# Second attention's routing steps behind the output, first expert slot loaded early, expert halves turned by DMA

## The reference

```
x = x + L1_xattn(_layernorm(x), ctx, ctx, Wq, bq, Wk, bk, Wv, bv, Wo)   # 16 heads of 64, 77 keys
x_flat = _layernorm(x).reshape(4096, 512)
topk_logits, topk_idx = top_k(x_flat @ moe_router, 2)                  # 8 experts, 2 per row
w = softmax(topk_logits)
x_sort = x_flat[token_ids_sort]                                        # rows sorted by expert
gate, up = split(ragged_dot(x_sort, moe_w13, group_sizes), 2)          # 512 -> 2 x 1024
out = ragged_dot(silu(gate) * up, moe_w2, group_sizes)                 # 1024 -> 512
x = x + zeros_like(x_flat).at[token_ids_sort].add(out * w_sort)
```

## Time and profile before

| | us |
|---|---|
| median of 3 runs | 2937.68 |
| lowest, highest | 2935.63, 2941.66 |
| the profiled execution's own time | 2946.32 |
| its span | 2944.4 |

### The profile page before, as it was taken

How to read it: one execution, slowest core, us unless ns; L and a number is a source line. 1 busy time by engine, 2 the same in 40 slices (tenths; PEclk the granted TensorE clock), 3 DMA queues, 4 the chain that set the end, 5 groups by cost and what they waited for, 6 DMA issues and landing times. The chain is left out here.

```text
span 2944.4 us, 45924 instructions
## 1 busy us (share of the span) xinstructions
PE 2430.0 (83%) x15743; PEld 1294.0 (44%) x15923; DVE 1664.0 (57%) x2533; ACT 1027.2 (35%) x1676; POOL 1094.7 (37%) x934
## 2 busy tenths in 40 slices
PE   8799944666656698888888499999999999999960
PEld 5566621222222265555555244444444444444430
DVE  4599878899898465555657442333333434342235
ACT  2365635788876444444445111111111111111100
POOL 0244412777767112323225650060633505330026
PEclk9799976889888799999999699999999999999985
DMA  6300013344333200111112331141322413231128
GB/s 238 120 2 2 2 58 118 130 177 164 118 118 118 75 10 10 38 38 34 38 48 80 111 108 36 29 120 30 114 78 75 118 32 97 74 82 29 36 83 277
DMA packets 181491, 240.15 MB, mean 82 GB/s; under 512 B 99110, under 2 KB 102182, under 8 KB 180854
## 3 DMA queue, kind: packets, MB, share of 16 engines
q1 hardware_dynamic: 158325, 158.73, 16.6%
q0 software_dynamic: 23040, 79.72, 8.7%
HBM read 101.77 MB, written 118.03 MB: 75 GB/s over the span
## 5 line engine op out<-in xcount | busy, mean ns | idle before, releaser
L2015 PE MATMUL e_gate_up<-weights,e_x_t 128*128 x3335 | 751.2, 380 | 28.1 <-DMA e_x_t<-sorted_x 23.9
L2015 PEld LDWEIGHTS e_gate_up<-weights,e_x_t 128*128 128x128 bf16 x3408 | 328.2, 98 | 394.7 <-issue 27.2
L2089 DVE TENSOR_TENSOR e_mid<-e_gate,e_gate_up 128x512 f32<-128x512 f32 x142 | 97.6, 687 | 574.1 <-ACT e_gate L2066 574.1
L2036 PE MATMUL e_out<-weights,e_mid_t 128*128 x1669 | 377.4, 379 | 4.3 <-issue 2.5
L2066 ACT ACTIVATE e_gate<-e_gate_up 128x512 f32<-128x512 f32 x142 | 84.8, 597 | 716.8 <-PE e_gate_up L2015 716.8
L2036 PEld LDWEIGHTS e_out<-weights,e_mid_t 128*128 128x128 bf16 x1704 | 166.7, 98 | 203.4 <-issue 2.9
L843 POOL TENSOR_TENSOR a_e<-a_e,a_total 128x616 f32<-128x616 f32 x64 | 76.4, 1214 | 405.6 <-DVE a_total L1202 405.6
L1510 POOL TENSOR_TENSOR f_shared<-f_shared 128x512 f32<-128x512 f32 x128 | 181.0, 1415 | 123.5 <-DVE f_shared L1788 123.5
L1580 PE MATMUL f_out<-f_w,hidden 128*128 128x512 f16 x512 | 141.3, 402 | 96.8 <-ACT hidden L1682 95.9
L1968 POOL TENSOR_TENSOR e_token<-e_token 1x1 f32<-1x1 f32 x6 | 1.1, 183 | 565.7 <-PE e_out L2036 565.7
L1499 POOL TENSOR_TENSOR hidden<-hidden,f_up_row 128x512 f32<-128x512 f32 x128 | 178.2, 1402 | 86.6 <-ACT f_up_row L1711 86.6
(11 more groups left out here) (262 smaller groups left out, 4089.9 us busy)
## 6 DMA issues: line engine op xcount, KB each, us to landing
sorted_x<-f_zero_row SPq DMA_DIRECT2D x8, 8448.0 KB, 24.1
raw_weights<-in_w POOLq DMA_DIRECT2D x88, 512.0 KB, 4.0
sorted_y<-e_y_rows SPq DMA_DIRECT2D x71, 256.0 KB, 2.0
x<-in_x SPq DMA_DIRECT2D x4, 2048.0 KB, 21.7
out<-x SPq DMA_DIRECT2D x32, 256.0 KB, 4.1
hidden<-in_w_t SPq DMA_DIRECT2D x1, 4096.0 KB, 17.3
f_shared<-in_w_t SPq DMA_DIRECT2D x1, 4096.0 KB, 13.3
weights<-in_w SPq DMA_DIRECT2D x6, 512.0 KB, 3.6
```

The costliest lines, as they stand in the source:

```text
L2015: last = nc.tensor.matmul(gate_up[half][:, part, :], x_t[:, u, a, k, :], plan.weights13[:, bass.ds(expert % 2, 1), b, k, col:col + 512], s ...
L2036: last = nc.tensor.matmul(out[:, :], mid_t[:, a, j, :], plan.weights2[:, bass.ds(expert % 2, 1), b, j, :], start=(j == 0 and a == b == 0), ...
L2089: nc.vector.tensor_tensor(mid[:, half, :], gate[:, half, :], gate_up[half][:, 1, :], ALU.mult).then_inc(mid_made, 1)
```

## The change

In `attention1` counts and partial logits come behind the output on TensorE; counts, while flips are made (before step `TAIL`), also behind the flips. Rows of all but the last two groups are turned, chosen and counted a step later than before (`begin`), while moments and norms keep their step. ScalarE normalises the rows ahead of the copy of the partial logits. VectorE adds the output before it does the routing's arithmetic, and `rows_of` copies the counts from PSUM into `counted` first, so that the bank is free at once.

The memory of the keys and of the turned expert rows is one (`plan.keys`, `plan.x_t`). SP issues the load of slot 0's rows at the end of `attention1`, once all scatters have landed; `experts` begins with the load of slot 1.

In `experts` TensorE no longer turns the middle. SP turns each half (128 x 1024 bf16, both parts) by a DMA transpose from `mid_parts` to `mid_t`, which has a second buffer (`mid_turn`). SP's order in slot s is: rows of slot s+2, results of slot s-1, the two halves of slot s. ScalarE copies the output of slot s-1 after VectorE has finished both halves of slot s, and VectorE waits for the turn of a half in the slot before ahead of overwriting it.

```diff
@@ -701,12 +703,14 @@
         for g, tiles in enumerate(GROUPS):
+            begin = tiles[-1] + (5 if g < len(GROUPS) - 2 else 4)
             norms_at[tiles[-1] + 4] = g
             for j in range(0, len(tiles), 2):
-                pairs_at[tiles[-1] + 4 + j // 2] = tiles[j]
-            choice_at[tiles[-1] + 4 + len(tiles) // 2] = g
-            rows_at[tiles[-1] + 5 + len(tiles) // 2] = g
+                pairs_at[begin + j // 2] = tiles[j]
+            choice_at[begin + len(tiles) // 2] = g
+            rows_at[begin + 1 + len(tiles) // 2] = g
         STEPS = NT + 6
+        TAIL = NT + 3
         groups_of = {t: g for g, tiles in enumerate(GROUPS) for t in tiles}
@@ -795,6 +799,11 @@
+            for i in range(SENT):
+                sp.wait_ge(sent_out[i], 32 * LATE // SENT)
+            sp.wait_ge(late_out, 32 * (NT - LATE))
+            sp.dma_start_transpose(out=plan.x_t[:, 0, :, :, :].rearrange("p a k n -> p (a k) n"),
+                                   in_=w["sorted_x"][0:P, :]).then_inc(plan.x_in[0], 16)
@@ -991,22 +1000,22 @@
                     turn(("turn", t))
-                if step in rows_at:
-                    counts(rows_at[step])
-                if step - 1 in pairs_at:
-                    parts_of(pairs_at[step - 1])
-                    if step > NT:
-                        logits_of(pairs_at[step - 1])
                 if step == 3:
...
                     output(step - 3)
+                if step in rows_at and step >= TAIL:
+                    counts(rows_at[step])
+                if step - 1 in pairs_at:
+                    parts_of(pairs_at[step - 1])
                 if 1 <= step <= NT:
...
                         flip(step - 1, q)
+                if step in rows_at and step < TAIL:
+                    counts(rows_at[step])
                 for t in route_turns(step):
                     turn(("route", t))
-                if step - 1 in pairs_at and step <= NT:
+                if step - 1 in pairs_at:
                     logits_of(pairs_at[step - 1])
@@ -1130,10 +1139,10 @@
                     turned(t)
+                for t in route_turns(step):
+                    norm(("route", t))
                 if step - 1 in pairs_at:
                     part_copy(pairs_at[step - 1])
-                for t in route_turns(step):
-                    norm(("route", t))
                 for q in range(QUARTERS if 1 <= step <= NT else 0):
@@ -1270,15 +1279,16 @@
-                amounts = bank(u)[:, 0:n * E].rearrange("p (i x) -> p i x", x=E)
-                above = bank(u)[:, TPS * E:(TPS + n) * E].rearrange("p (i x) -> p i x", x=E)
+                amounts, above = counted[:, 0:n, :], counted[:, n:2 * n, :]
...
+                nc.vector.tensor_copy(counted[:, 0:2 * n, :], bank(u)[:, 0:2 * n * E].rearrange(
+                    "p (i x) -> p i x", x=E)).then_inc(unit_low, 1)
+                dve.wait_ge(unit_low, low[u])
...
-                nc.vector.tensor_tensor(run[:, 0:n, :], run[:, 0:n, :], above, ALU.add).then_inc(unit_low, 1)
-                dve.wait_ge(unit_low, low[u])
+                routed(nc.vector.tensor_tensor(run[:, 0:n, :], run[:, 0:n, :], above, ALU.add))
@@ -1351,16 +1361,13 @@
                     norms(norms_at[step])
-                if step in rows_at:
-                    rows_of(rows_at[step])
-                if step > NT:
-                    route(step)
                 if 3 <= step < NT + 3:
...
                         moments(norms_at[step + 1])
-                if step <= NT:
-                    route(step)
+                if step in rows_at:
+                    rows_of(rows_at[step])
+                route(step)
                 for c in projections(step):
@@ -1856,6 +1863,10 @@
+        self.keys = sb("keys", [P, 2, 2, D // 64, KEYS], BF16)
+        self.x_t = self.keys[:, :, :, :, :].rearrange("p b a c n -> p (b a c n)")[:, 0:4 * KD * P].rearrange(
+            "p (u a k n) -> p u a k n", u=2, a=2, k=KD)
+        self.x_in = [stack.enter_context(nc.semaphore(f"x_in{i}")) for i in range(2)]
@@ -1990,17 +1999,31 @@
-            for s in range(2):
-                x_load(s, s)
+            x_load(1, 1)
+
+            def mid_turn(s, u, half):
+                sp.dma_start_transpose(out=mid_t[:, u, half, :, :, :].rearrange("p a j n -> p (a j) n"),
+                                       in_=mid_parts[:, half, :, :].rearrange("p a n -> p (a n)")
+                                       ).then_inc(mid_turned[half][u], 16)
+
+            def y_store(s, u):
+                sp.dma_start(sorted_y[bass.ds(s * P, P), :], y_rows[:, u, :]).then_inc(y_out[u], 16)
...
-                sp.wait_ge(out_copied, s + 1)
-                sp.dma_start(sorted_y[bass.ds(s * P, P), :], y_rows[:, u, :]).then_inc(y_out[u], 16)
+                if first:
+                    sp.wait_ge(mid_low, 2)
+                else:
+                    sp.wait_ge(out_copied, s)
+                    y_store(s - 1, 1 - u)
+                mid_turn(s, u, 0)
+                mid_turn(s, u, 1)
...
+            sp.wait_ge(out_copied, SLOTS)
+            y_store(SLOTS - 1, (SLOTS - 1) % 2)
@@ -2018,22 +2041,14 @@
-            def flip_mid(s, half):
-                pe.wait_ge(mid_low, 2 * s + half + 1)
-                at_least(pe, mid_copied, 2 * s + half - 1)
-                for j in range(MC):
-                    last = nc.tensor.transpose(mid_flip[half][:, j * P:(j + 1) * P],
-                                               mid_parts[:, half, j // 4, j % 4 * P:(j % 4 + 1) * P],
-                                               core.ident_bf[:, :])
-                last.then_inc(mid_flipped, 1)
-
-            def output(s, expert):
+            def output(s, u, expert):
...
-                pe.wait_ge(mid_copied, 2 * s + 2)
+                for half in range(2):
+                    pe.wait_ge(mid_turned[half][u], 16 * (s // 2 + 1))
...
-                        last = nc.tensor.matmul(out[:, :], mid_t[:, a, j, :],
+                        last = nc.tensor.matmul(out[:, :], mid_t[:, u, j // (MC // 2), a, j % (MC // 2), :],
@@ -2047,16 +2062,12 @@
                 half_products(s, u, 0, expert)
-                if not first:
-                    flip_mid(s - 1, 1)
                 half_products(s, u, 1, expert)
                 if not first:
-                    output(s - 1, expert_of(s - 1))
-                flip_mid(s, 0)
+                    output(s - 1, 1 - u, expert_of(s - 1))
             slots(pe, slot)
-            flip_mid(SLOTS - 1, 1)
-            output(SLOTS - 1, expert_of(SLOTS - 1))
+            output(SLOTS - 1, (SLOTS - 1) % 2, expert_of(SLOTS - 1))
@@ -2065,50 +2076,42 @@
-            def out_copy(s, u):
+            def out_copy(s, u, last):
...
+                if not last:
+                    act.wait_ge(mid_low, 2 * s + 4)
...
-                    out_copy(s - 1, 1 - u)
+                    out_copy(s - 1, 1 - u, False)
...
-            out_copy(SLOTS - 1, (SLOTS - 1) % 2)
+            out_copy(SLOTS - 1, (SLOTS - 1) % 2, True)
...
-            def multiply(s, half):
+            def multiply(s, u, half):
...
-                at_least(dve, mid_flipped, n - 1)
+                if not isinstance(s, int) or s >= 1:
+                    dve.wait_ge(mid_turned[half][1 - u], 16 * ((s + 1) // 2))
...
-            def mid_copy(s, half):
-                dve.wait_ge(mid_flipped, 2 * s + half + 1)
-                if half == 0:
-                    at_least(dve, out_ready, s)
-                nc.vector.tensor_copy(mid_t[:, :, half * MC // 2:(half + 1) * MC // 2, :],
-                                      mid_flip[half][:, :].rearrange("p (a j n) -> p a j n", a=2, j=MC // 2)
-                                      ).then_inc(mid_copied, 1)
-
...
-                multiply(s, 0)
-                if not first:
-                    mid_copy(s - 1, 1)
-                multiply(s, 1)
-                mid_copy(s, 0)
+                multiply(s, u, 0)
+                multiply(s, u, 1)
```

27 lines of the change are left out of this document (13 added, 14 removed).

## The result

| kernel | median of 4 | lowest to highest | profiled execution, its span | clock over the span |
|---|---|---|---|---|
| before | 2939.66 us | 2935.63 to 2941.66 | 2946.32, 2944.4 | 0.920 |
| changed | 2824.67 us | 2822.25 to 2827.31 | 2822.83, 2821.1 | 0.927 |

The ratio is 0.9611, with a 95% interval of 0.9594 to 0.9627: 115 us less. The median lies 12 us above the forecast of 2813, inside the stated range of 2788 to 2862.

What follows compares the result with a forecast made beforehand. TensorE, busy 83% of the span, was taken to bound the stages touched. 62.3 + 8.5 - 6 + 41 + 12 + 7 = 124.8 us off 2946.3 gives 2821.5; against the median, 8.6 us lower, 2813; range 2788 to 2862, own range 2790 to 2832.

Steps and rivals of the forecast that it cites:

- The flips: Experts' stage: 70 slots each lose two sets of flips on TensorE, 0.445 us a set, 62.3 us gained.
- The chain through SP: Experts, T = previous output's end: turns land by T + 6.1, needed T + 10.4; k, price against rows' load, free below 1.9.
- the cover for the turns: Experts: two matmul groups of the next slot run ahead of the output, leaving 4.3 us slack, so turns cost nothing.
- rival 2: Experts: turns late only beside weight loads, 0.6 us in a third of slots, some 15 us with scatter: 2828; chance 0.08.
- outputs wait for them: Experts: a sign that the prediction is wrong, TensorE's outputs waiting for the DMA turns; no size given.
- Rival 1: Experts: DMA turn dear and the bound, 3150 us at k = 3; chance 0.12 beyond k = 2.3, 0.04 from 1.9 to 2.3.
- Start: Start of the experts' stage: first load lands inside GpSimd's drain, so TensorE starts sooner; 8.5 us gained.
- End: Last experts' slot: nothing covers its turns, 3.8 us more, and the clock may add up to 5.2; 6 us lost.
- The attention: Second attention: 41 us from waits that go, plus 12 us from less time at 1.2 GHz, bounds 0 and 18.
- All three waits: Second attention, TensorE: ring bank 19.0 us, flips on ScalarE's copies 14.9, flips on VectorE's rows arithmetic 7.8; all go.
- rival 3: Second attention: removed waits give place to new ones, only 25 of the 60 us come: 2848; chance 0.15.
- The end of the routing: Behind 1582, the last batch: waits on counts and rows arithmetic, 8.4 us at most, 7 gained; the choice gives some back.

Runs made afterwards that it cites:

- changed_again: The changed kernel itself, run once more on another chip: 2829.76 us, ratio 0.9616 to the kernel before.
- early_only: The kernel before with only the load of the first slot's rows behind the last scatters and the shared buffers: 2932.18 us, ratio 0.9978.
- turns_only: The kernel before with only the experts' edit, the middle turned by DMA; attention and first load as before: 2884.32 us, ratio 0.9820.
- attention_only: The kernel before with only the second attention's edits, no early load, flips still on TensorE: 2884.39 us, ratio 0.9817.

## Why the prediction was right, and where not

**The flips, 62.3 us:** right to the digit. The slot is 15.54 us instead of 16.43, 0.89 x 70 = 62.3. The wait of 2.4 us at the first output was in no term. With it and the last slot the experts' stage should be 54.8 us shorter, and it is 54.6.

**The chain through SP at k = 1:** right. T + 1.6 for T + 1.5, landed at T + 6.2 for T + 6.1. The threshold was not: "below k = 1.9 it is free" is true of the slots without loads alone. Two idle turns should have kept 1.6 us of slack; they cost 68 us, nearly all beside weight loads. The step that failed is the cover for the turns, which I took as 4.3 us nearly everywhere; for turns late beside loads rival 2 had 15 us. Issue and landing both stretch there, and the outputs behind late turns ran at a lower clock as well (7.22 us in changed_again instead of 5.35). In the change as it stands the margin mostly suffices; three of nine profiled executions had one slot in which it didn't. That is what rival 2 was about, and it was worth 5 to 7 us where it came. By the prediction's own signs of being wrong, "outputs wait for them" is so at three outputs of 71. Rival 1, the dear turn, is refuted at k = 1, and its price of 0.46 us a slot for each 0.1 of k was too low, as it left the clock and the loads out.

**The ends.** Start: 8.5 forecast. From the first instruction of GpSimd after its drain to TensorE's first matmul it was 9.4 us and is 1.3, 8.1 less:

```profile
1595.93 0.96 POOL L843 DMA_INDIRECT sorted_x<-weights,plan_rows  x1 [0.30 <-issue]
1598.69 1.36 SPq L805 DMA_TRANSPOSE keys<-sorted_x  x1
1604.42 0.09 POOL L1949 MEMSET e_token<- 1x3 f32 x1 [7.53 <-POOLq L599]
...
1605.74 2.74 PE L2038 MATMUL e_gate_up<-weights,keys 128*128 x6 [19.74 <-POOL e_token L1956]
```

The load lies in the drain as said, and TensorE's releaser is now GpSimd's announcement. Only 5.2 us of the median arrived in early_only (the interval holds 3.8 to 9.4). With the load behind the barrier TensorE started 8.5, 6.6 and 7.6 us after its issue in before, turns_only and attention_only, so I had priced the slowest of the three. End: 6 lost, measured 5.1: from the start of the last flips to the last copy it was 7.6 us (2838.18 to 2845.8), and from the end of the output before to the last copy it is 12.7. Of that the clock cost 1.3 us (24 matmuls in 6.66 for 5.35), not up to 5.2, and the wait 3.8, as forecast.

**The attention, 41 + 12 us:** the total is nearly right, the terms are not. All three waits went, 37.7 us in 1130 to 1530. Two errors offset each other: I had no new wait, and one of 6.2 us came (the kind that rival 3 describes, 6.2 us where that rival had 35; a new wait at the turned rows was also one of the signs of being wrong); and I took 12 of the clock's 18, while the clock is 1.00 from 1130 to 1530. The assignment was off too. The 14.9 us of the flips on ScalarE are shown to come from the turned rows; of the ring bank's waits laid to the partial logits' place, less than half returns when they are put back, 7.6 of 17.0 us.

**The end of the routing, 7 us:** mis-sized. From the last scores to the last counts it was 67.1 us (1582.28 to 1649.37) and is 65.7 (1520.04 to 1585.78): 1.4. The waits moved more than they went. TensorE waited for normalised rows 5.8 us in one, and now 7.4 in three:

```profile
1557.36 1.12 PE L886 MATMUL a_ring<-ident,a_xn 128*128 128x128 f32 x4 [4.93 <-ACT a_xn L1040]
...
1560.77 7.54 PE L984 MATMUL a_out<-weights 128*128 128x512 bf16 x24
```

and in the kernel before, from its waits at 1582 to 1660 and its timeline:

```profile
PE a_ring L877 <- ACT a_xn L1031: 5.8, 1, 5.8
...
1615.00 7.73 PE L975 MATMUL a_out<-weights 128*128 128x512 bf16 x23 [0.26 <-issue]
```

ScalarE's norm waits at 1557 for GpSimd's splits, which stand behind the scatters of the step. The output behind it takes 7.5 us at the lower clock, and the kernel before had such an output too. VectorE adds one copy of 4.93 us that the kernel before did not have (last section). Then the last rows are ready at 1588.84, but their scatters start at 1592.01, since GpSimd is still busy with the scatters and splits of the tiles before; in the kernel before the last scatters began 0.3 us behind their rows. From the last counts to GpSimd's first instruction behind its drain it was 14.7 us and is 18.6. So the whole end of the routing is 2.6 us longer than before, where 7 were to be gained. I had written that the choice "gives some back", and not asked what GpSimd had queued. That its queue is the cause is read from the trace and was not tried.

**The level.** The profiled executions differ by 123.5 us, the sum was 124.8; but 3.8 of these lie ahead of the second attention's scores (they begin at 1014.0 and 1010.2), in code that is the same. In medians the parts brought 53.0 where the steps say 56.3, 53.0 for 60, and 5.2 for 8.5, 111 for 125. From the level I had taken 8.6 us off for the long profiled execution of before. Its surplus lay partly in the stages whose waits I counted (attention 569.1 us, against 565.9 and 568.4 with the same code), so a part of the 8.6 us was in the sum already. The stages themselves gave 119.0 us (58.4, 6.0 and 54.6) of the 124.8. How the 12 us between forecast and median divide between the two was not tried. That the sum came so near is partly luck: an end of the routing 9.6 us worse than its term stands against an attention some 5 better than its own. The forecast's own range, 2790 to 2832, does not follow from the bounds named with it, which give 2803 to 2835; the median lies in both.

## What to carry to other kernels

Price the slack of a new transfer in the busiest stretch of its queues, not in the median: by the formula two more transposes took 2.7 us of a slack of 4.3, and wherever weights were loaded nothing was left. A step moved later on one engine shifts work on the engines that follow it, so list what GpSimd or ScalarE has queued at the new place, above all where the loop runs out. Give the first and the last round of a loop, where nothing covers the turns, an order of their own: it was worth 8 us here. And taking one move back from the finished kernel shows what it is worth beside the others, which can be more or less than it gained on the kernel before.
